# A selective scan beside a mixture of experts on one core: one of eight C products per step goes to GpSimd, small copies go to ScalarE, the preparation of dt moves half a step earlier

## The chip, the core and the metric

The kernel runs on one core of a Trainium2 chip. A core has five engines that run their own instruction streams in order and meet through semaphores: TensorE (PE, with its weight loads PEld), VectorE (DVE), ScalarE (ACT), GpSimd (POOL) and SyncE (SP), which here only issues DMAs. The metric is the device time of one execution in microseconds (us). Before the change the median of three executions is 4128.31 us (4123.35 to 4130.89).

## The reference, cut to what matters

All of it is in float32. Two branches work on the layer-normalised rows `xn` (16 x 1024 rows of 256) and are added to `x`.

```
x  = L0_attn_x                       # (16, 1024, 256)
xn = layernorm(x)
# branch 1: a selective scan, 32 states for each of 256 channels
dt = softplus(xn @ dt_w + dt_b);  b = xn @ B_w.T + B_b;  c = xn @ C_w.T + C_b
A  = -exp(log_A)                                     # (256, 32)
h_t = exp(A * dt_t) * h_(t-1) + (dt_t * x_t) * b_t   # (256, 32) for each row t
y_t = sum over states of h_t * c_t  +  D_skip * x_t
# branch 2: mixture of experts, 8 experts, 2 chosen per row, capacity 4096 rows each
out_e = relu(disp_e @ w1_e + b1_e) @ w2_e + b2_e;    moe_t = sum of 2 gates * out[expert, slot]
return x + y + moe
```

## The kernel before

A first part (about 370 us) normalises the rows, writes them to `xn_rows`, transposes them, routes them to experts and prepares dt, dt*x, b and c of the first batch entry. The rest is one loop of 128 steps, and everything below is about that loop. A batch entry has 1024 rows, done in two halves of 512 columns (`HALF`), and a half takes 4 steps (`ng` = 0 to 3). One step does two things side by side.

*The scan.* A step covers 8 groups of states (`k` = 0 to 7), each with two tiles (`dh` = 0, 1) of 128 partitions (4 states x 32 channels) by 512 rows. For one tile ScalarE computes the decay `exp(a*dt)` into PSUM (`decay`, line 734), GpSimd has multiplied `u = dtx * b` for both tiles of a k (line 935), and VectorE runs the scan over the 512 rows (line 1154). Then VectorE multiplies both tiles of h with c (`weigh`, line 1138, into `hc`), and TensorE sums the states of two k at a time into PSUM (`quad(s)` for k = 2s and 2s+1, line 569). There are two PSUM tiles for decays, so `decay` of a (k, dh) waits for the scan of (k-1, dh). `u` has four buffers, so GpSimd's product for k waits for the scans of k-4. h is a ring of four k and hc another: `weigh(k)` writes where k-4 stood and waits for the quad that read it.

*The experts.* Each step takes 256 slots of an expert: GpSimd gathers their rows (line 878), TensorE transposes them (`turn_slots`), multiplies with w1 (`moe_up(0..3)`, line 607) and w2 (`moe_down(0..1)`, line 623), ScalarE moves each PSUM tile on (`up_out`, line 769; `down_out`, line 778), and GpSimd scatters the result into the output in the next step with an adding DMA (line 895). GpSimd also adds y to the output (line 900, four DMAs per half, one per step) and forms the two small gate operands (lines 952 and 957).

*The preparation.* Each step also prepares 128 rows for a later half: TensorE's `prep` (line 527), ScalarE's `evac_prep`, `softplus` and `log_part` (lines 711 to 725), VectorE's `prep_dt` (line 1063), GpSimd's `dtx_part` (line 857), and SP stores them.

The order of each stream is written out by hand in Python loops; there is no scheduler. What matters below is what stands behind what. On TensorE one step is moe_up(0), moe_up(1), quad(0), moe_up(2), moe_up(3), quad(1), moe_down(0), prep, quad(2), moe_down(1), turn_slots, quad(3). On ScalarE the decays of k+1 follow the scans of k, and between them stand the other tasks by their k: `down_out(0)` stands behind the decays that follow k = 5, and so ahead of both decays for k = 7. On VectorE `weigh(k-1)` stands behind the first scan of k.

## Time and profile before

| | before |
|---|---|
| median of three executions | 4128.31 us |
| profiled execution, its own time | 4136.54 us |
| profiled execution, its span | 4134.7 us |
| VectorE busy | 3945.4 us (95%) |
| GpSimd busy | 3438.1 us (83%) |
| TensorE busy | 3386.1 us (82%) |
| ScalarE busy | 2479.6 us (60%) |
| mean granted TensorE clock | 0.915 |

The span runs from the first to the last instruction of the profiled execution. Busy time is an average over the set-up and the loop, and says nothing about which engine a step ends on; for that the time line of a single step has to be read. On GpSimd the record of an instruction can begin while the one before it still runs, so the mean duration of a group is longer than what one instruction adds to the engine's time. There the distance between two ends is the number to use.

### The profile page before, as it was taken

To read this page: it belongs to the slowest core of one execution; us is meant where nothing else is said; L and a number is where in the kernel's file an instruction comes from. 1 tells how busy PE (TensorE), PEld (TensorE's weight loads), DVE (VectorE), ACT (ScalarE), POOL (GpSimd) and SP (SyncE) were. 2 spreads that over 40 slices of the span, in tenths; PEclk is the share of its full clock that TensorE was granted. 3 is DMA by queue.
4 is the path that set the end of the run, shared out by engine and by line. 5 is a ranking of instruction groups with operands and counts; after the bars stand their busy time and mean duration, and the time that the engine had idled before them with its cause. 6 is when DMAs were issued, how large, how long until landed. Compare 5 with 4: busy or idle time off the path is not lost.

```text
span 4134.7 us, 75470 instructions
## 1 busy us (share of the span) xinstructions
PE 3386.1 (82%) x16264; PEld 2230.3 (54%) x16264; DVE 3945.4 (95%) x4035; ACT 2479.6 (60%) x5211; POOL 3438.1 (83%) x2340
## 2 busy tenths in 40 slices
PE   6788888878888888888888888888888888888786
PEld 3366555555555555555555555555555555555554
DVE  8797999999999999999999999999999999999997
ACT  2302666666666666666666666666666666666665
POOL 3003999989999899989998898988998999989997
PEclk8998999999999999999999999999999999999998
DMA  7983554445544454445554444445554544545554
GB/s 231 340 145 88 112 122 104 105 111 129 126 113 115 110 120 105 106 111 129 122 117 112 112 116 103 111 110 129 120 120 105 117 107 109 116 110 131 120 120 107
DMA packets 405229, 510.41 MB, mean 123 GB/s; under 512 B 71855, under 2 KB 242995, under 8 KB 404595
## 3 DMA queue, kind: packets, MB, share of 16 engines
q1 hardware_dynamic: 310774, 404.45, 36.0%
q0 software_dynamic: 68976, 84.86, 13.7%
q10 hardware_dynamic: 25104, 16.91, 1.8%
q8 instruction: 136, 2.23, 0.2%
q14 instruction: 239, 1.96, 0.2%
HBM read 381.48 MB, written 142.08 MB: 127 GB/s over the span
## 4 chain that ended last, share of the span: by engine, by line
DVE 32%; issue 15%; ACT 15%; PE 11%; POOL 11%; DVEq 4%; SPq 3%; DMA 3%; ACTq 1%; POOLq 0%
DVE h L1154 19%; ACT bank L734 11%; DVE hc L1138 10%; POOL u L935 6%; PE bank L623 4%; POOL out_rows L895 4%; PE bank L607 3%; DVEq L1154 3%; PE bank L569 2%; SPq L341 2%; ACT bank L785 2%; DMA dt<-dt_rows 1%; DVE hc L1116 1%; SPq L328 1%; ACT zv L711 1%
## 5 line engine op out<-in xcount | busy, mean ns | idle before, releaser
L935 POOL TENSOR_TENSOR u<-dtx,b_sb 128x1024 f32<-128x1024 f32 x1024 | 2656.9, 2785 | 139.3 <-DVE h L1154 125.4
L1154 DVE TENSOR_TENSOR_SCAN h<-bank,carry,u 128x512 f32<-128x512 f32 x2048 | 2541.1, 1276 | 107.9 <-ACT bank L734 81.0
L734 ACT ACTIVATE bank<-dt,a_neg 128x512 f32<-128x512 f32 x2050 | 1412.8, 690 | 1110.8 <-DVE h L1154 1048.9
L1138 DVE TENSOR_TENSOR hc<-h,bank 128x1024 f32<-128x1024 f32 x1024 | 1232.9, 1204 | 4.4
L607 PE MATMUL bank<-xgt,w_sb 128*128 128x256 f32 x4096 | 1109.7, 431 | 65.1 <-ACT ht L769 51.5
L607 PEld LDWEIGHTS bank<-xgt,w_sb 128*128 128x128 f32 x4096 | 871.8, 219 | 453.7 <-issue 317.3
L569 PE MATMUL bank<-hc,rsum 128*32 128x512 f32 x4096 | 618.7, 679 | 565.5 <-DVE hc L1138 563.2
L623 PE MATMUL bank<-w_sb,ht 128*128 128x256 f32 x4096 | 984.9, 395 | 0.0
L623 PEld LDWEIGHTS bank<-w_sb,ht 128*128 128x128 f32 x4096 | 780.2, 196 | 328.1 <-issue 226.2
L769 ACT ACTIVATE ht<-bank,b_sb 128x256 f32<-128x256 f32 x1024 | 423.8, 465 | 173.6 <-PE bank L607 160.8
L569 PEld LDWEIGHTS bank<-hc,rsum 128*32 128x32 f32 x4096 | 83.8, 112 | 752.2 <-DVE hc L1138 724.4
L895 POOL DMA_INDIRECT out_rows<-o_sb,sidx x258 | 414.7, 1607 | 66.4 <-issue 58.5
L857 POOL TENSOR_TENSOR dtx_n<-dt_n,xnt 128x256 f32<-128x256 f32 x136 | 173.9, 1279 | 300.5 <-DVE dt_n L1063 300.5
L878 POOL DMA_INDIRECT xg<-xn_rows,gidx x256 | 277.5, 1084 | 156.0 <-DVE h L1154 114.9
L900 POOL DMA_DIRECT2D out_rows<-y_sb x133 | 200.4, 1522 | 7.3 <-DMA out_rows<-o_sb,sidx 7.3
L785 ACT ACTIVATE bank<-c_sb 128x512 f32<-128x512 f32 x256 | 151.1, 590 | 14.5 <-DVE hc L1138 13.8
L711 ACT ACTIVATE zv<-bank,dtb 128x128 f32<-128x128 f32 x272 | 83.0, 356 | 126.4 <-PE bank L527 99.5
L527 PE MATMUL bank<-xnt,dtw 128*128 x1096 | 158.0, 287 | 0.0
L778 ACT ACTIVATE o_sb<-bank,gate 128x256 f32<-128x256 f32 x256 | 117.0, 457 | 51.7 <-PE bank L626 49.2
L527 PEld LDWEIGHTS bank<-xnt,dtw 128*128 128x128 f32 x1096 | 132.8, 191 | 17.0 <-issue 1.6
L554 PE MATMUL bank<-hc,u 128*128 128x256 f32 x512 | 119.3, 391 | 13.3 <-DVE hc L1116 13.3
L885 POOL COPY sidx<-slot_dst 128x2 int32 x129 | 121.3, 940 | 0.0
(109 smaller groups left out, 1960.6 us busy)
## 6 DMA issues: line engine op xcount, KB each, us to landing
dt<-dt_rows SPq DMA_DIRECT2D x528, 128.0 KB, 4.0
dtx<-dtx_rows SPq DMA_DIRECT2D x528, 128.0 KB, 3.4
b_sb<-bc_rows SPq DMA_DIRECT2D x520, 128.0 KB, 3.3
c_sb<-bc_rows SPq DMA_DIRECT2D x520, 128.0 KB, 3.5
w_sb<-w SPq DMA_DIRECT2D x18, 1024.0 KB, 7.6
dt_rows<-dt_n SPq DMA_DIRECT2D x136, 128.0 KB
dtx_rows<-dtx_n SPq DMA_DIRECT2D x136, 128.0 KB
out_rows<-y_sb POOLq DMA_DIRECT2D x133, 128.0 KB, 3.8
```

The source lines that it names most:

```text
L527: mm = pe.matmul(dst, w[:, k, :], src, start=(k == 0), stop=(k == KD - 1))
L569: mm = pe.matmul(y_ps[c * RD:(c + 1) * RD, s % 2, :], rsum[:], hc[:, 2 * (k % HB) + dh, :], start=False, stop=True, skip_group_check=True, ...
L607: mm = pe.matmul(m[:, c * SL:(c + 1) * SL], w1_sb[:, eo, kk, ch * P:(ch + 1) * P], xgt[:, kk, :], start=(kk == 0), stop=(kk == KD - 1))
L623: pe.matmul(m[:, 0:D], ht[:, c, j * P:(j + 1) * P], w2_sb[:, eo, c, :], start=(c == 0), stop=False)
L734: act.activation(a_ps[dh], dt[:, g, :], ACT.Exp, scale=a_neg[:, bass.ds(col, 1)]).then_inc(a_ready, 1)
L769: ins = act.activation(ht[:, ch, :], m_ps[f % 2][:, c * SL:(c + 1) * SL], ACT.Relu, bias=b1_sb[:, bass.ds(e * HC + ch, 1)])
L785: act.activation(c_ps, c_sb[:, ng % 2, jj, :], ACT.Copy).then_inc(c_ready, 1)
L878: pool.indirect_dma_start(xg[:, j, :], None, xn_d, rows, bounds_check=T - 1, oob_is_err=False).then_inc(xg_in, 16)
L895: pool.indirect_dma_start(outf, rows, o_sb[:, buf, j, :], None, bounds_check=T - 1, oob_is_err=False, compute_op=ALU.add).then_inc(o_scatt ...
L935: pool.tensor_tensor(u[:, 2 * i:2 * i + 2, :], dtx[:, 2 * gp:2 * gp + 2, :], b_sb[:, odd, k // 4, :].unsqueeze(1).to_broadcast([P, KD, HALF]),
L1138: dve.tensor_tensor(hc[:, 2 * (k % HB):2 * (k % HB) + 2, :], h[:, 2 * k % HR:2 * k % HR + 2, :], c_ps.unsqueeze(1).to_broadcast([P, KD, HA ...
L1154: dve.tensor_tensor_scan(h[:, (2 * k + dh) % HR, :], a_ps[dh], u[:, 2 * (k % UB) + dh, :], carry[:, bass.ds(hh % 2, 1), bass.ds(ng * 2 * N ...
```

## The change

1. The product of h with c for k = 3 (`HP = 3`) is done by GpSimd and no longer by VectorE. GpSimd reads c from SBUF. It stands behind GpSimd's u product for k = 7. VectorE's first scan of k = 7 waits for it (it overwrites those tiles of h), and so does TensorE's quad(1).
2. The gate products and the copies of the index columns `gidx` and `sidx` go from GpSimd to ScalarE, behind its decays of k = 2 (gates, gather index) and k = 6 (scatter index). The gate products become four activations of one column.
3. The four adding DMAs of y per half, of 128 rows each, become one of 512 rows, in the step with `ng` = 1.
4. The gathered rows have two buffers. The gathers stand behind GpSimd's k = 0 and k = 1, the scatters behind k = 4 and 5, `dtx_part` behind k = 3.
5. The preparation moves by about half a step: `prep` stands ahead of quad(1) on TensorE, `evac_prep` at k = 4, softplus at 5 and the logarithm at 6 on ScalarE, `prep_dt` behind the last scan of the step on VectorE. One more block is prepared ahead of the loop.
6. SP's stores and loads follow suit; `load_c` also waits for GpSimd's product.

```diff
@@ tensor @@
                             def quad(s):
-                                pe.wait_ge(hc_done, st * NG + 2 * s + 1 + 2)
+                                pe.wait_ge(hc_done, st * (NG - 1) + 2 * s + 1 - (2 * s + 1 >= HP) + 2)
+                                if s == HP // 2:
+                                    pe.wait_ge(hcp_done, st + 1)
                                 sum_states(s)
...
                                 quad(0)
                                 moe_up(2)
                                 moe_up(3)
+                                prepare()
                             quad(1)
                             moe_down(0)
-                            pe.wait_ge(xnt_in, 16 * (nx // HPB + 2))
-                            settle(pe)
-                            prep(NG + nx, 1 - nx // NG % 2, nx % NG)
                             quad(2)
@@ scalar @@
+                        def gates_in():
+                            act.wait_ge(xg_in, 16 * SJ * (st + 1))
+                            settle(act)
+                            for j in range(SJ):
+                                ins = act.activation(gate2[:, j:j + 1], xg[:, ng % 2, j, D + 1:D + 2], ACT.Copy,
+                                                     scale=slot_k[:, bass.ds(st * SJ + j, 1), 1])
+                            ins.then_inc(gate_mul, 1)
+                            act.wait_ge(gate_mul, st + 1)
+                            settle(act)
+                            for j in range(SJ):
+                                ins = act.activation(gate[:, j:j + 1], xg[:, ng % 2, j, D:D + 1], ACT.Identity,
+                                                     scale=slot_k[:, bass.ds(st * SJ + j, 1), 0], bias=gate2[:, j:j + 1])
+                            ins.then_inc(gate_ready, 1)
...
+                                if k == 5:
+                                    softplus(p)
+                                if k == 6:
+                                    log_part(p)
...
                             if k == 2:
-                                softplus(p)
-                                log_part(p)
+                                gates_in()
+                                lay_gather()
                             if k == 3:
                                 up_out(3)
+                            if k == 6:
+                                lay_scatter()
+                            if k == 4:
+                                evac_prep(p)
                             if k == 5:
                                 down_out(0)
@@ gpsimd @@
-            def add_y(hf, j):
-                pool.dma_start(outf.rearrange("(i p) d -> i p d", p=P)[bass.ds(hf * TB + j, 1)]
-                               .rearrange("a p d -> (a p) d"), y_sb[:, j, :], accum_op=ALU.add).then_inc(y_out, 16)
+            def add_y(hf):
+                pool.dma_start(groups(outf)[bass.ds(hf, 1)].rearrange("a p j d -> (a p) j d"), y_sb[:],
+                               accum_op=ALU.add).then_inc(y_out, 16)
...
+                            if k < 2:
+                                gather(st + 1, 1 - odd, k)
                             if k == 3:
                                 dtx_part(p, par, q)
+                            if k in (4, 5):
+                                scatter(st, 1 - odd, k - 4, hf + 1 if ng == 1 else None)
+                            if k == UB + HP:
+                                pool.wait_ge(c_in[odd], 16 * R * (hf * HPB // 2 + ng // 2 + 1))
+                                pool.wait_ge(nsum_done, st * 4 + HP // 2 - 2 + 1 + NSUM0)
+                                pool.wait_ge(scan_done, st * 2 * NG + 2 * HP + 2 + SCAN0)
+                                pool.tensor_tensor(hc[:, 2 * HP:2 * HP + 2, :], h[:, 2 * HP:2 * HP + 2, :],
+                                                   c_sb[:, odd, 0, :].unsqueeze(1).to_broadcast([P, KD, HALF]),
+                                                   ALU.mult).then_inc(hcp_done, 1)
@@ vector @@
+            prep_dt(NG)
...
+                                if (k, dh) == (HP + UB, 0):
+                                    dve.wait_ge(hcp_done, st + 1)
...
-                                if dh == 0 and k > 0:
+                                if dh == 0 and k > 0 and k - 1 != HP:
                                     weigh(st, k - 1)
-                            if k == 3:
-                                prep_dt(NG + st)
+                        prep_dt(NG + 1 + st)
                         weigh(st, NG - 1)
```

The first place is GpSimd in a step, from k = 5 on. This is before:

```order
L957 TENSOR_TENSOR gate<-gate 128x2
L873 REGISTER_ALU
L878 DMA xg<-xn_rows,gidx 128x258
L933 REGISTER_ALU
L935 TENSOR_TENSOR u<-dtx,b_sb 128x1024
L878 DMA xg<-xn_rows,gidx 128x258
L892 REGISTER_ALU
L895 DMA out_rows<-o_sb,sidx 16384x256
L933 REGISTER_ALU
L935 TENSOR_TENSOR u<-dtx,b_sb 128x1024
L895 DMA out_rows<-o_sb,sidx 16384x256
```

Now, from its u product for k = 4 on:

```order
L971 TENSOR_TENSOR u<-dtx,b_sb 128x1024
L924 ISA
L929 DMA out_rows<-o_sb,sidx 16384x256
L969 REGISTER_ALU
L971 TENSOR_TENSOR u<-dtx,b_sb 128x1024
L929 DMA out_rows<-o_sb,sidx 16384x256
L969 REGISTER_ALU
L971 TENSOR_TENSOR u<-dtx,b_sb 128x1024
L969 REGISTER_ALU
L971 TENSOR_TENSOR u<-dtx,b_sb 128x1024
L988 ISA
L990 TENSOR_TENSOR hc<-h,c_sb 128x1024
```

The h-by-c product (line 990) is the last of the step and has all four u products of k = 4 to 7 and both scatters ahead of it; the gate addition (line 957) and the gathers are gone from this stretch.

The second place is TensorE between moe_up(3) (lines 607 and 613) and moe_down(0) (lines 623 and 629), in a step with `ng` above 0. Before, with `rsum` marking a quad and `dtw` and `bcw` the preparation:

```order
L607 MATMUL bank<-xgt,w_sb 128x256 x4
L630 REGISTER_ALU
L569 MATMUL bank<-hc,rsum 32x512 x4
L615 REGISTER_ALU
L623 MATMUL bank<-w_sb,ht 128x256 x6
L621 REGISTER_ALU
L623 MATMUL bank<-w_sb,ht 128x256 x2
L626 MATMUL bank<-b_p,ones 128x256
L649 ISA
L521 REGISTER_ALU
```

Now:

```order
L613 MATMUL bank<-xgt,w_sb 128x256 x4
L527 REGISTER_ALU
L533 MATMUL bank<-xnt,dtw 128x128 x4
L533 MATMUL bank<-xnt,bcw 64x128 x2
L575 MATMUL bank<-hc,rsum 32x512 x4
L621 REGISTER_ALU
L629 MATMUL bank<-w_sb,ht 128x256 x6
L627 REGISTER_ALU
L629 MATMUL bank<-w_sb,ht 128x256 x2
L632 MATMUL bank<-b_p,ones 128x256
L575 MATMUL bank<-hc,rsum 32x512 x4
```

The preparation went ahead of quad(1); quad(1) still stands ahead of the whole of moe_down(0).

The third place is ScalarE in the same step around `down_out(0)` (the activation into `o_sb`). Before, from the decays for k = 6:

```order
L734 ACTIVATE bank<-dt,a_neg 128x512
L790 REGISTER_ALU
L734 ACTIVATE bank<-dt,a_neg 128x512
L775 ISA
L777 REGISTER_ALU
L778 ACTIVATE o_sb<-bank,gate 128x256
L822 ACTIVATE carry<-h 128x4
L790 REGISTER_ALU
L734 ACTIVATE bank<-dt,a_neg 128x512
```

Now (the decay is line 750 here):

```order
L750 ACTIVATE bank<-dt,a_neg 128x512
L732 ACTIVATE za<-zv 128x256
L734 ACTIVATE ze<-za 128x256
L830 REGISTER_ALU
L750 ACTIVATE bank<-dt,a_neg 128x512
L792 REGISTER_ALU
L793 ACTIVATE o_sb<-bank,gate 128x256
L868 ACTIVATE carry<-h 128x4
L830 REGISTER_ALU
L750 ACTIVATE bank<-dt,a_neg 128x512
L738 ACTIVATE bank<-ze 128x256
```

Parts of softplus came in, and `down_out(0)` stands where it stood: ahead of the first decay for k = 7.

## Rows read from the trace of the kernel before

**Rows 1.** Costliest groups of the page: line, engine, operation | busy us, mean ns | idle before.
```profile
L935 POOL TENSOR_TENSOR u<-dtx,b_sb 128x1024 f32<-128x1024 f32 x1024 | 2656.9, 2785 | 139.3 <-DVE h L1154 125.4
L1154 DVE TENSOR_TENSOR_SCAN h<-bank,carry,u 128x512 f32<-128x512 f32 x2048 | 2541.1, 1276 | 107.9 <-ACT bank L734 81.0
```

**Rows 2.** Time line of VectorE: start us, length us, what [idle before <-releaser].
```profile
397.97 0.42 DVE L1063 SCALAR_TENSOR_TENSOR dt_n<-zv,bank 128x256 f32<-128x256 f32 x1
...
2073.93 3.62 DVE L1154 TENSOR_TENSOR_SCAN h<-bank,carry,u 128x512 f32<-128x512 f32 x3
...
2080.96 1.20 DVE L1138 TENSOR_TENSOR hc<-h,bank 128x1024 f32<-128x1024 f32 x1
...
2085.55 1.28 DVE L1154 TENSOR_TENSOR_SCAN h<-bank,carry,u 128x512 f32<-128x512 f32 x1
2086.74 0.40 DVE L1063 SCALAR_TENSOR_TENSOR dt_n<-zv,bank 128x256 f32<-128x256 f32 x1
...
2096.31 2.46 DVE L1154 TENSOR_TENSOR_SCAN h<-bank,carry,u 128x512 f32<-128x512 f32 x2
...
2099.79 1.29 DVE L1154 TENSOR_TENSOR_SCAN h<-bank,carry,u 128x512 f32<-128x512 f32 x1
...
2102.26 3.63 DVE L1154 TENSOR_TENSOR_SCAN h<-bank,carry,u 128x512 f32<-128x512 f32 x3
```

**Rows 3.** All writers of dt_n: length min/median/max ns, first and last start.
```profile
L1063 DVE SCALAR_TENSOR_TENSOR dt_n<-zv,bank x136: 396/403/464, 246.8 to 4097.6; 128x256 f32<-128x256 f32 x136
```

**Rows 4.** Time line of GpSimd over a part of two steps.
```profile
2111.93 1.14 POOL L878 DMA_INDIRECT xg<-xn_rows,gidx  x1 [1.05 <-DVE h L1154]
...
2118.06 2.93 POOL L935 TENSOR_TENSOR u<-dtx,b_sb 128x1024 f32<-128x1024 f32 x1
2121.17 1.59 POOL L895 DMA_INDIRECT out_rows<-o_sb,sidx  x1 [0.17 <-DVE h L1154]
2122.20 1.31 POOL L857 TENSOR_TENSOR dtx_n<-dt_n,xnt 128x256 f32<-128x256 f32 x1
2122.89 7.57 POOL L935 TENSOR_TENSOR u<-dtx,b_sb 128x1024 f32<-128x1024 f32 x3
2129.82 1.55 POOL L900 DMA_DIRECT2D out_rows<-y_sb  x1
```

**Rows 5.** Time line of TensorE in the step of rows 2.
```profile
2082.21 1.94 PE L569 MATMUL bank<-hc,rsum 128*32 128x512 f32 x8 [3.42 <-DVE hc L1138]
2084.07 4.36 PE L607 MATMUL bank<-xgt,w_sb 128*128 128x256 f32 x16
2089.50 1.06 PE L569 MATMUL bank<-hc,rsum 128*32 128x512 f32 x8 [1.07 <-DVE hc L1138]
2094.15 0.28 PE L626 MATMUL bank<-b_p,ones 3*128 x1
2095.45 0.65 PE L527 MATMUL bank<-xnt,bcw 128*64 x4
```

**Rows 6.** Time line of ScalarE behind that moe_down(0).
```profile
2094.79 0.45 ACT L778 ACTIVATE o_sb<-bank,gate 128x256 f32<-128x256 f32 x1
2095.33 0.69 ACT L734 ACTIVATE bank<-dt,a_neg 128x512 f32<-128x512 f32 x1
```

**Rows 7.** Time lines of TensorE, ScalarE and VectorE in a step with ng = 0.
```profile
2031.38 1.94 PE L569 MATMUL bank<-hc,rsum 128*32 128x512 f32 x8 [2.81 <-DVE hc L1138]
2033.25 5.86 PE L623 MATMUL bank<-w_sb,ht 128*128 128x256 f32 x16
...
2039.35 0.47 ACT L778 ACTIVATE o_sb<-bank,gate 128x256 f32<-128x256 f32 x1 [2.62 <-PE bank L626]
...
2040.79 1.28 DVE L1154 TENSOR_TENSOR_SCAN h<-bank,carry,u 128x512 f32<-128x512 f32 x1 [1.30 <-ACT bank L734]
```

**Rows 8.** Time lines of TensorE and ScalarE around one preparation ahead of the loop.
```profile
344.57 1.09 PE L527 MATMUL bank<-xnt,dtw 128*128 x8
...
347.93 0.39 ACT L725 ACTIVATE bank<-ze 128x256 f32<-128x256 f32 x1
```

More of the change, by code:

```diff
@@ L154, in ssm_moe @@
         sidx = sb("sidx", [P, SJ], I32)
-        xg = sb("xg", [P, SJ, D + 2])
-        gate2 = sb("gate2", [P, SJ, 2])
+        xg = sb("xg", [P, 2, SJ, D + 2])
+        gate2 = sb("gate2", [P, SJ])
+        HP = 3
         gate = sb("gate", [P, SJ])
@@ L443, in _ @@
                         settle(sp)
+                        sp.wait_ge(hcp_done, st + 1)
+                        settle(sp)
                         load_c(ng % 2, st + 2)
-                        store_dtx(p, par, q)
+                        nxt = hh * HPB + ng + 1
+                        store_bc(p + 1, (1 + nxt // NG) % 2, nxt % NG)
                         if last:
@@ L730, in _ @@
                 log_part(q)
+            evac_prep(NG)
+            softplus(NG)
+            log_part(NG)
             def decay(dh, col, g):
@@ L877, in gather @@
                 rows = bass.IndirectOffsetOnAxis(ap=gidx[:, j:j + 1], axis=0)
-                pool.indirect_dma_start(xg[:, j, :], None, xn_d, rows,
+                pool.indirect_dma_start(xg[:, buf, j, :], None, xn_d, rows,
                                         bounds_check=T - 1, oob_is_err=False).then_inc(xg_in, 16)
-            def lay_scatter(st):
-                pool.wait_ge(o_scattered, 16 * SJ * (st + 1))
-                settle(pool)
-                pool.tensor_copy(sidx[:], slot_dst[:, bass.ds(st * SJ, SJ)]).then_inc(sidx_done, 1)
             def scatter(st, buf, j, added):
                 if j == 0:
-                    pool.wait_ge(sidx_done, st + 2)
+                    pool.wait_ge(sidx_done, st + 1)
                     pool.wait_ge(evac_done, st * FS + 1)
-                    pool.wait_ge(y_out, 16 * added)
+                    if added is not None:
+                        pool.wait_ge(y_out, 16 * added)
                     settle(pool)
@@ L908, in _ @@
                 rows = bass.IndirectOffsetOnAxis(ap=gidx[:, j:j + 1], axis=0)
-                pool.indirect_dma_start(xg[:, j, :], None, xn_d, rows,
+                pool.indirect_dma_start(xg[:, 0, j, :], None, xn_d, rows,
                                         bounds_check=T - 1, oob_is_err=False).then_inc(xg_in, 16)
+            pool.wait_ge(xg_in, 16 * SJ)
+            pool.tensor_copy(gidx[:], slot_tok[:, 2 * SJ:3 * SJ]).then_inc(gidx_done, 1)
             pool.wait_ge(map_ready, 2)
@@ L937, in _ @@
                                                ALU.mult).then_inc(u_ready, 1)
-                            if k == 2:
-                                pool.wait_ge(y_evac, hf + (2 if ng > 0 else 1))
+                            if k == 0 and ng == 1:
+                                pool.wait_ge(y_evac, hf + 2)
                                 pool.wait_ge(o_scattered, 16 * SJ * (st + 1))
                                 settle(pool)
-                                if ng > 0:
-                                    add_y((hf + 2 * B - 1) % (2 * B), ng - 1)
-                                else:
-                                    add_y((hf + 2 * B - 2) % (2 * B), TB - 1)
+                                add_y((hf + 2 * B - 1) % (2 * B))
@@ L955, in _ @@
-                            if k == 5:
-                                pool.wait_ge(gate_mul, st + 1)
-                                pool.tensor_tensor(gate[:], gate2[:, :, 0], gate2[:, :, 1], ALU.add).then_inc(gate_ready, 1)
-                                gather(st + 1, 0)
-                            if k == 6:
-                                gather(st + 1, 1)
-                                scatter(st, 1 - odd, 0, st + 1)
-                            if k == 7:
-                                scatter(st, 1 - odd, 1, st + 1)
-                                dtx_part(p, par, q)
@@ L966, in _ @@
-            pool.wait_ge(o_scattered, 16 * SJ * (STEPS + 1))
-            add_y(2 * B - 2, TB - 1)
-            lay_scatter(STEPS)
+                                dtx_part(p, par, q)
+                            if k in (4, 5):
[7 more added lines that the diff above has]
+                                                   ALU.mult).then_inc(hcp_done, 1)
@@ L969, in _ @@
             for j in range(SJ):
-                scatter(STEPS, 1, j, STEPS + 1)
+                scatter(STEPS, 1, j, None)
             pool.wait_ge(o_scattered, 16 * SJ * (STEPS + 2))
             pool.wait_ge(y_evac, 2 * B + 2)
-            for j in range(TB):
-                add_y(2 * B - 1, j)
-            pool.wait_ge(y_out, 16 * (STEPS + 1 + TB))
+            add_y(2 * B - 1)
+            pool.wait_ge(y_out, 16 * (2 * B + 1))
             pool.wait_ge(xg_in, 16 * SJ * (STEPS + 1))
```

70 lines of the change are left out of this document (35 added, 35 removed).

## The prediction

> **What bounds the kernel now.** I read the page's first and fifth part, then the time line of one step on VectorE, then those of the engines that VectorE waits for, then the same in a step that was longer. The page says that VectorE is 95% busy and that its scan group sat idle for 107.9 us in all, 81.0 of them for ScalarE's decays [rows 1]. On the time line a step without a stall runs from the scan at 2073.93 to the one at 2102.26, which is 28.33 us [rows 2]; it holds 16 scans of 1.18 us (3.63 for three, less the 0.10 by which records overlap), 8 weighs of 1.11 and the 0.31 of dt_n. The first dt_n of the loop starts at 397.97 [rows 2] and the last at 4097.6 [rows 3], 127 steps apart, so a mean step is (4097.6 - 397.97)/127 = 29.13 us. So 0.80 us per step are stalls, and VectorE sets the time. If GpSimd takes one weigh, VectorE needs 28.33 - 1.11 = 27.22.
>
> GpSimd is the next to look at. Three u products end 7.57 - 0.62 = 6.95 us after dtx_n ends (2123.51 to 2130.46), which is 2.32 each [rows 4], not the 2.785 of the page [rows 1]; the records overlap the instruction ahead. A scatter behind a product adds 1.77 (2120.99 to 2122.76), dtx_n 0.75 (2122.76 to 2123.51), a gather 1.14 and about 0.17 ahead of it, and the first gather has 1.05 us of idle time ahead of it, for the gate it waits for [rows 4].
>
> **The change part by part.** The h-by-c product has the shape and operands (two in SBUF) of u, so I take 2.35 us for it; it and u are the same form, and between u's own extremes there is little room (2.32 when back to back, 2.37 at most with a wait ahead). GpSimd's step is then 9 products, 21.0, two gathers 2.5, two scatters 3.55 and dtx_n 0.75: 27.8 us, plus add_y. It loses four tiny instructions (0.13 each) and the 1.05 of idle time. So GpSimd alone could run a step in 27.8, VectorE in 27.2, both under 28.33. That would be the gain. It is lost to order.
>
> Follow h of k = 3. Call t the end of its second scan (2085.55 + 1.28 = 2086.83 in the step shown [rows 2]). Before, weigh(3) followed within one scan, TensorE started quad(1) at 2089.50, the last matmul of moe_down(0) ended at 2094.43, ScalarE's down_out(0) started at 2094.79 and the first decay for k = 7 ended at 2096.02 [rows 5, 6], 1.46 us before its scan began at 2096.31 + 1.17 = 2097.48 [rows 2]. Now GpSimd must do u for k = 7 and the product, 4.7 us and 0.2 for the wait: the product ends at t + 4.9 at the earliest, call that T. From T on everything is in order behind one another: quad(1) and moe_down(0) 4.93 (2089.50 to 2094.43), down_out(0), carry and decay 1.2 (2094.79 to 2096.02), and the hand-overs 0.1 from GpSimd and 0.28 to VectorE (2039.35 + 1.16 = 2040.51 to 2040.79 [rows 7]). That is 6.5 us from T to the first scan of k = 7. Between t and that scan VectorE now has six scans and two weighs, 6 x 1.18 + 2 x 1.11 = 9.3, so it would start it at t + 9.3. It can start it at t + 4.9 + 6.5 = t + 11.4. VectorE waits 2 us in every step, behind k = 6, for ScalarE, and the 1.42 us saved are gone.
>
> Now close the circle. From the first scan of k = 7 to the first scan of the next step is 2102.26 - 2097.48 = 4.78 [rows 2], and 0.31 for dt_n, which moves there: 5.09. The next u for k = 4 waits for both scans of k = 0: 5.09 + 2.46 + 0.2 = 7.75. From there GpSimd has u 2.35, scatter 1.77, u 2.35, scatter 1.77, u 2.32, u 2.32, the product 2.35: 15.3, so the next product ends 23.1 behind the first scan of k = 7. The step is 23.1 + 6.5 = 29.6 us. With GpSimd always on time it would be 5.09 + 12.90 (2073.93 to 2086.83) + 4.9 + 6.5 = 29.4, so GpSimd is late by 0.2 only. Against the mean of 29.13 the loop loses 0.47 x 128 = 60 us. The present stalls of 0.80 us do not come on top: those behind k = 4 to 6 fall into the new 2 us wait, and the longer work of TensorE at ng = 0 into its wait for the product.
>
> add_y: four DMAs of 1.55 us become one, of which no row has the size. From below it costs no more than one of 128 rows, 1.55 [rows 4]; from above four times that, 6.2. Between T and the u of k = 4 GpSimd has 3 x 2.32 + 2.6 = 9.5 ahead of u for k = 3, which may start at 6.5 + 3.6 + 0.2 = 10.3, and ends with dtx_n at 13.4 where the next u may start at 14.25: 1.7 us of room. At 1.55 it costs nothing, at 6.2 it costs 4.5 x 32 = 144 us. I take 2.5, nearest to the row that is there, and 0.8 x 32 = 26 us. By the Trainium skill, DMA: Bandwidth & Descriptors, Anatomy of one DMA, descriptor generation is small and many descriptors can be emitted before more of them cost anything; by that this term would be 0. No row here has two sizes to test it.
>
> TensorE's clock: quad(1) takes 1.06 us where the engine idled 1.07 ahead, and 1.94 with 2.81 or 3.42 of idle time ahead; behind the 2.81 the moe_down took 5.86 us, and from quad(1) to the scan it was 2040.79 - 2031.38 = 9.41 us [rows 5, 7], 2.8 more than the warm 6.6. That step is also the model of what I expect: VectorE stalled for 1.30 us there for the same decay [rows 7]. In the new order TensorE is through with the preparation 5.09 + 8.23 (end of weigh(1), 2082.16 [rows 2]) + 6.2 + 1.8 = 21.3 behind the first scan of k = 7 (quad(0) to moe_up(3) 2082.21 to 2088.43 [rows 5]), the product comes at 23.1, so it idles 1.8, nearer to the 1.07. With add_y in the step it is 2.6 and may go either way; I take a quarter of 32 x 2.8, some 20 us.
>
> Gates and index copies on ScalarE: about 6 x 0.2 us, where the softplus of 1.3 us left; each decay behind them has its scan a group later, so nothing. If that cover were gone it would be 0.2 x 128 = 26 us. The second gather buffer takes a wait for moe_up(0) off the gathers and costs nothing. SP's load_c waits for the product, with half a step and more in hand; nothing. Ahead of the loop one preparation more stands between the last count and the slot maps: 344.57 to 348.32 on TensorE and ScalarE [rows 8], 3.75, and dt_n, hand-overs and a store: 6 us.
>
> Sum: 60 + 26 + 20 + 6 = 112 on the profiled execution's own 4136.5 (its span is 4134.7). That execution is 8.2 us over the median of 4128.3, so the forecast is 4128.3 + 112 = 4240.
>
> **The rivals.** *GpSimd's sum decides and nothing is late (faster).* A step of 27.8 and add_y 2.5/4 = 0.6 gives 28.4: 0.73 x 128 = 93 less and 6 more, 4041. It holds if the product is out by t + 2.9, so that the decay for k = 7 is where VectorE wants it. For it: GpSimd's sum and VectorE's are both below 28.33. Against it: u for k = 7 alone takes until t + 2.5, and the three orders all put moe_down(0) behind quad(1) and the decay behind down_out(0).
>
> *No change.* The circle at its shortest, 29.4, no add_y, no cold quad: 0.27 x 128 + 6 = 41 above before at most; to come to nothing TensorE would have to pass from quad(1) to the last matmul in 4.6 in place of 4.93. For it: quad(2) and quad(3) steps run at the full clock. Against: the 4.93 are at the full clock already.
>
> *The cold circle (slower by more).* The idle time ahead of quad(1) is enough to drop the clock in most steps, from 2.4 to 1.2 GHz. Then 2.8 us come on top in each such step. At add_y 6.2 and in a quarter of the steps: 4128 + 60 + 144 + 90 + 6 = 4428. In all steps it would be over 4500. For it: 2.81 us of idle time did it in [rows 7]. Against: the 1.8 us I work out.
>
> **How the numbers follow.** Forecast and its neighbours, 4165 to 4320: 0.60. Faster rival: 0.15. No change and little more, 4120 to 4165: 0.12. Cold circle or dear add_y, above 4320: 0.13. The range for 8 in 10 leaves out most of the first rival and the worst of the last: 4085 to 4350. Below 0.2% (8 us) no change can be told from none: faster 0.16, same 0.06, slower 0.78.
>
> **What would show it.** In the profile after, the scan of k = 7 has about 2 us of idle time ahead, released by ScalarE's decay, in nearly every step, 200 us and more in all; ScalarE's down_out(0) waits for TensorE in nearly every step; quad(1) waits for GpSimd's product. The step is 29.6 where dt_n starts are compared. VectorE's busy time falls by 128 x 1.2 = 154 us and its share to about 90%. The product takes 2.35 us. I am wrong if VectorE's idle time stays below 100 us, if the product stands behind less than u for k = 7, or if add_y takes over 3 us.

## The result, and the profile after

| | before | after |
|---|---|---|
| median | 4125.83 us | 4357.20 us |
| ratio to before, 95% interval | | 1.0552 (1.0536 to 1.0568) |
| profiled execution, span | 4134.7 us | 4358.9 us |
| VectorE busy | 3945.4 us (95%) | 3808.9 us (87%) |
| GpSimd busy | 3438.1 us | 3581.2 us |
| mean granted TensorE clock | 0.915 | 0.897 |

The change makes the kernel 5.5% slower; the medians are 231 us apart, the two profiled executions 224 us (4358.9 against 4134.7). The sign and the place were as forecast, but the loss is twice the 112 us of the sum, and 7 us beyond the range.

Costliest groups of the page after. The first line answers to that of VectorE's scan in [rows 1]:

```profile
L1181 DVE TENSOR_TENSOR_SCAN h<-bank,carry,u 128x512 f32<-128x512 f32 x2048 | 2534.3, 1270 | 474.4 <-ACT bank L750 448.4
L971 POOL TENSOR_TENSOR u<-dtx,b_sb 128x1024 f32<-128x1024 f32 x1024 | 2579.9, 2550 | 339.4 <-DVE h L1181 320.8
L1163 DVE TENSOR_TENSOR hc<-h,bank 128x1024 f32<-128x1024 f32 x896 | 1073.1, 1198 | 0.0
L793 ACT ACTIVATE o_sb<-bank,gate 128x256 f32<-128x256 f32 x256 | 118.8, 464 | 444.7 <-PE bank L632 428.4
L990 POOL TENSOR_TENSOR hc<-h,c_sb 128x1024 f32<-128x1024 f32 x128 | 325.2, 2540 | 0.0
```

ScalarE's `down_out` before, from the same part of the page:

```profile
L778 ACT ACTIVATE o_sb<-bank,gate 128x256 f32<-128x256 f32 x256 | 117.0, 457 | 51.7 <-PE bank L626 49.2
```

VectorE has 128 products fewer, and its idle time ahead of scans went from 107.9 to 474.4 us, nearly all of it until a decay of ScalarE. ScalarE's `down_out`, which waited 51.7 us in the kernel before, now waits 444.7, for TensorE. And GpSimd itself waits for VectorE, 320.8 us: in this kernel no engine's own work is the bound.

The chain in one step is the one to look at. Time lines of the changed kernel on VectorE, GpSimd, TensorE and ScalarE, one fence each:

```profile
2116.25 1.28 DVE L1181 TENSOR_TENSOR_SCAN h<-bank,carry,u 128x512 f32<-128x512 f32 x1 [2.41 <-ACT bank L750]
...
2142.39 1.28 DVE L1181 TENSOR_TENSOR_SCAN h<-bank,carry,u 128x512 f32<-128x512 f32 x1
2147.21 1.28 DVE L1181 TENSOR_TENSOR_SCAN h<-bank,carry,u 128x512 f32<-128x512 f32 x1 [3.54 <-ACT bank L750]
```
```profile
2131.66 5.22 POOL L971 TENSOR_TENSOR u<-dtx,b_sb 128x1024 f32<-128x1024 f32 x2
2136.64 2.54 POOL L990 TENSOR_TENSOR hc<-h,c_sb 128x1024 f32<-128x1024 f32 x1
...
2141.24 1.60 POOL L934 DMA_DIRECT2D out_rows<-y_sb  x1
```
```profile
2108.28 1.52 PE L575 MATMUL bank<-hc,rsum 128*32 128x512 f32 x8 [1.97 <-POOL hc L990]
2109.73 4.91 PE L629 MATMUL bank<-w_sb,ht 128*128 128x256 f32 x16
...
2139.23 1.75 PE L575 MATMUL bank<-hc,rsum 128*32 128x512 f32 x8 [4.07 <-POOL hc L990]
2140.91 4.68 PE L629 MATMUL bank<-w_sb,ht 128*128 128x256 f32 x16
2145.53 0.28 PE L632 MATMUL bank<-b_p,ones 3*128 x1
```
```profile
2145.84 0.47 ACT L793 ACTIVATE o_sb<-bank,gate 128x256 f32<-128x256 f32 x1 [4.93 <-PE bank L632]
2146.21 0.20 ACT L868 ACTIVATE carry<-h 128x4 f32<-128x4 f32 x1
2146.31 0.68 ACT L750 ACTIVATE bank<-dt,a_neg 128x512 f32<-128x512 f32 x1
```

Read them as a circle. From the first scan of k = 7 (2116.25) to the end of GpSimd's product (2139.18) it is 22.93 us. TensorE begins quad(1) 0.05 later, ends moe_down(0) at 2145.81, ScalarE takes down_out(0), carry and the decay, and the next scan of k = 7 begins at 2147.21, 8.03 behind the product: 30.96 us in all. VectorE was ready for it 3.54 us earlier. The two quads show the part that I mis-sized: with 1.97 us of idle time ahead quad(1) took 1.52 us, with 4.07 it took 1.75, and the moe_down behind it 4.9 and 4.7. In the step of [rows 5] quad(1) took 1.06 at 2.4 GHz, and the moe_down behind it, in the kernel before, 3.72:

```profile
2090.50 3.72 PE L623 MATMUL bank<-w_sb,ht 128*128 128x256 f32 x16
```

The granted clock of the changed kernel was 0.58 of full speed from 2139.2 to 2141.0 and 0.80 from 2141.0 to 2145.8.

The mean step, from the first dt_n of the loop to the last (all writers of dt_n in the second fence), is (4341.9 - 423.25)/127 = 30.86 us against 29.13:

```profile
419.75 1.28 DVE L1181 TENSOR_TENSOR_SCAN h<-bank,carry,u 128x512 f32<-128x512 f32 x1 [9.31 <-ACT bank L750]
...
423.25 0.39 DVE L1087 SCALAR_TENSOR_TENSOR dt_n<-zv,bank 128x256 f32<-128x256 f32 x1
```
```profile
L1087 DVE SCALAR_TENSOR_TENSOR dt_n<-zv,bank x137: 392/396/421, 245.9 to 4341.9; 128x256 f32<-128x256 f32 x137
```

127 x 1.73 = 220 us of the 224 between the two profiled executions lie between these marks, and 5 us ahead of the first dt_n and behind the last: the stretch ahead grew from 397.97 to 423.25 us, mostly since dt_n now stands at the end of its step, and the one behind shrank from 37.1 to 17.0. In the very first step the chain held the scan of k = 7 back by 9.31 us.

### The profile page after: what moved, and what is told of

Its sections match the earlier page's. It is cut to its first block, busy times and chain, and to the rows that moved or that the text cites. A ratio compares the mean times of both kernels' runs of the same rounds, so it can differ in the third digit from the quotient of the medians.

```text
span 4358.9 us, 74834 instructions
## 1 busy us (share of the span) xinstructions
PE 3471.6 (80%) x16264; PEld 2278.4 (52%) x16264; DVE 3808.9 (87%) x3908; ACT 2612.1 (60%) x5985; POOL 3581.2 (82%) x1856
## 4 chain that ended last, share of the span: by engine, by line
PE 23%; issue 23%; DVE 19%; POOL 18%; ACT 11%; DVEq 2%; DMA 2%; SPq 1%; ACTq 0%; POOLq 0%
DVE h L1181 14%; PE bank L629 11%; POOL u L971 10%; ACT bank L750 6%; POOL hc L990 6%; PE bank L575 5%; PE bank L613 3%; DVE hc L1163 3%; PE bank L560 3%; ACT ht L784 2%; POOL out_rows L929 2%; DMA dt<-x 1%; DVEq L1181 1%; DVE h L1055 1%; ACT bank L738 1%
## 5 line engine op out<-in xcount | busy, mean ns | idle before, releaser
L1181 DVE TENSOR_TENSOR_SCAN h<-bank,carry,u 128x512 f32<-128x512 f32 x2048 | 2534.3, 1270 | 474.4 <-ACT bank L750 448.4
L971 POOL TENSOR_TENSOR u<-dtx,b_sb 128x1024 f32<-128x1024 f32 x1024 | 2579.9, 2550 | 339.4 <-DVE h L1181 320.8
L575 PE MATMUL bank<-hc,rsum 128*32 128x512 f32 x4096 | 670.8, 731 | 759.0 <-DVE hc L1163 473.9
L613 PE MATMUL bank<-xgt,w_sb 128*128 128x256 f32 x4096 | 1083.4, 422 | 15.4 <-issue 11.8
L1163 DVE TENSOR_TENSOR hc<-h,bank 128x1024 f32<-128x1024 f32 x896 | 1073.1, 1198 | 0.0
L629 PE MATMUL bank<-w_sb,ht 128*128 128x256 f32 x4096 | 1067.7, 419 | 0.0
L629 PEld LDWEIGHTS bank<-w_sb,ht 128*128 128x128 f32 x4096 | 841.5, 211 | 385.7 <-issue 262.2
L793 ACT ACTIVATE o_sb<-bank,gate 128x256 f32<-128x256 f32 x256 | 118.8, 464 | 444.7 <-PE bank L632 428.4
L903 POOL TENSOR_TENSOR dtx_n<-dt_n,xnt 128x256 f32<-128x256 f32 x136 | 99.7, 733 | 299.7 <-DVE dt_n L1087 299.7
L990 POOL TENSOR_TENSOR hc<-h,c_sb 128x1024 f32<-128x1024 f32 x128 | 325.2, 2540 | 0.0
L533 PE MATMUL bank<-xnt,dtw 128*128 128x128 f32 (+1 forms) x1096 | 148.0, 278 | 0.0
L560 PEld LDWEIGHTS bank<-hc,u 128*128 128x128 f32 x512 | 95.5, 193 | 35.7 <-DVE hc L1140 23.6
```

Of the source, the lines that this page charges most:

```text
L533: mm = pe.matmul(dst, w[:, k, :], src, start=(k == 0), stop=(k == KD - 1))
L560: pe.matmul(map_ps, oh_p[:, r, :], oh_c[:, r, :], start=False, stop=True, skip_group_check=True).then_inc(oh_used, 1)
L575: mm = pe.matmul(y_ps[c * RD:(c + 1) * RD, s % 2, :], rsum[:], hc[:, 2 * (k % HB) + dh, :], start=False, stop=True, skip_group_check=True, ...
L613: mm = pe.matmul(m[:, c * SL:(c + 1) * SL], w1_sb[:, eo, kk, ch * P:(ch + 1) * P], xgt[:, kk, :], start=(kk == 0), stop=(kk == KD - 1))
L629: pe.matmul(m[:, 0:D], ht[:, c, j * P:(j + 1) * P], w2_sb[:, eo, c, :], start=(c == 0), stop=False)
L971: pool.tensor_tensor(u[:, 2 * i:2 * i + 2, :], dtx[:, 2 * gp:2 * gp + 2, :], b_sb[:, odd, k // 4, :].unsqueeze(1).to_broadcast([P, KD, HALF]),
```

## The experiments

All times are medians in us; "step" is the mean distance of dt_n starts in the profiled execution. e11_early and e12_product_alone were timed once and have no ratio. The kernel before was timed again beside each group.

| kernel | time | ratio to before | step |
|---|---|---|---|
| before | 4126 to 4133 | | 29.13 |
| after | 4357.20 | 1.0552 | 30.86 |
| e1_warm | 4222.21 | 1.0220 (1.0203 to 1.0237) | 29.79 |
| e2_swap | 4091.39 | 0.9903 (0.9886 to 0.9919) | 28.81 |
| e3_late_out | 4184.25 | 1.0127 (1.0110 to 1.0144) | 29.52 |
| e4_first | 4121.23 | 0.9972 (0.9959 to 0.9984) | 29.02 |
| e5_back | 4124.27 | 0.9996 (0.9984 to 1.0008) | 29.02 |
| e8_swap_early | 4062.69 | 0.9845 (0.9829 to 0.9862) | 28.51 |
| e10_back_early | 4070.75 | 0.9862 (0.9844 to 0.9881) | 28.64 |
| e11_early | 4393.40, one run | | 31.12 |
| e12_product_alone | 4803.14, one run | | 34.37 |
| e13_swap_early_dt | 4036.93 | 0.9769 (0.9753 to 0.9786) | 28.36 |
| e14_swap_early_dt_first | 4022.95 | 0.9732 (0.9716 to 0.9748) | 28.24 |

### e1_warm: fill TensorE's wait with work

```diff
-            def prep(p, par, q):
+            def prep(p, par, q, reps=1):
...
-                for g in range(3):
+                for g in list(range(3)) * reps:
...
-                                prep(NG + 1 + st, (1 + nxt // NG) % 2, nxt % NG)
+                                prep(NG + 1 + st, (1 + nxt // NG) % 2, nxt % NG, 3 if ng == 0 else 2)
```

> The changed kernel with the matmuls of the preparation ahead of quad(1) issued twice (three times where ng = 0), the same values each time: 1.7 us (3.4 us) more work for TensorE per step, laid into its wait for GpSimd's product. Theory (the missing 1.4 us per step are the clock that falls in that wait): quad(1) takes 1.06 in place of 1.5 to 1.75 us, moe_down(0) 3.7 in place of 4.7 to 4.9, from the end of the product to the first scan of k = 7 it is 6.5 in place of 8.0 us, the step falls from 30.9 to about 29.5 and the time to about 4185. Rival (TensorE is simply too full or late in the new order, the clock is not the cause): more work makes it no faster, 4357 to 4450.

135 us less by doing more. Time line of TensorE:

```profile
2136.49 0.65 PE L533 MATMUL bank<-xnt,bcw 128*64 128x128 f32 x4
2137.62 1.07 PE L575 MATMUL bank<-hc,rsum 128*32 128x512 f32 x8 [0.48 <-POOL hc L990]
2138.61 3.72 PE L629 MATMUL bank<-w_sb,ht 128*128 128x256 f32 x16
2142.27 0.28 PE L632 MATMUL bank<-b_p,ones 3*128 x1
```

quad(1) and moe_down(0) are back at 2.4 GHz (granted clock 1.00 from 2137.6 to 2142.5): 4.93 us from the start of the one to the end of the other. From the product to the scan of k = 7 the median is 6.48 us, against 8.12 in the changed kernel, and from that scan to the next product it stays (22.91 against 22.88). The median step is 29.38 us, the 29.4 of the circle with GpSimd on time.

The mean is 29.79, so the time came out 37 us above the expected 4185. In 37 steps the way from the product to the scan of k = 7 is longer, by 34 us in all, mostly since stalls of about 2.4 us ahead of the scans of k = 4 and 5 outlast the wait for the product; another 21 us lie between the scan and the product over the ends of the halves. The clock is the missing part, and the rival is out.

### e11_early: the same work, laid elsewhere

```diff
                             moe_up(1)
+                            if ng > 0:
+                                prepare()
...
-                                prepare()
                             quad(1)
```

> The changed kernel with the preparation ahead of quad(0) where ng is above 0, quad(1) still ahead of moe_down(0): the same work, moved. Theory (the clock in the wait for the product is the missing part of the step): the idle time ahead of quad(1) grows by the 1.7 us of the preparation, quad(1) takes 1.94 and moe_down(0) 5 to 6 us, the circle is 22.9 + 9.4 = 32.3 us in three steps of four, time 4480 to 4560. Rival (a constant hand-over or another order costs the missing part, not the clock): unchanged, 4340 to 4370, or faster as e8_swap_early was.

4393 is between the two. Time line of TensorE:

```profile
2119.31 1.06 PE L575 MATMUL bank<-hc,rsum 128*32 128x512 f32 x8 [3.43 <-POOL hc L991]
2120.31 5.41 PE L629 MATMUL bank<-w_sb,ht 128*128 128x256 f32 x16
```

Over each kernel I took the idle time ahead of the quad that waited for the product, and the time from its start to the end of moe_down(0), as medians over the 89 such steps of e1_warm and all 128 of the others:

| kernel | idle ahead | quad(1) to end of moe_down(0) |
|---|---|---|
| e1_warm | 0.43 us | 4.93 us |
| after | 1.98 | 6.57 |
| e11_early | 5.06 | 6.54 |
| e12_product_alone | 6.76 | 6.71 |

The medians hide two kinds of steps. In the changed kernel 31 of the 128 waits ahead of quad(1) were under 1.8 us, 17 of them in steps with ng = 1, and behind none of them was anything lost (4.93 us). Behind all of the other 97 it took 6.5 us or more, with 1.8 to 2.4 us ahead as with 4. In e11_early 125 of 128 steps lost that much. So the low clock mostly costs 1.6 to 1.8 us, with 2 us idle as with 7, and up to 3.1 in single steps (15 of 128 in e11_early lost more than 2); the 2.8 that I had read from one step in [rows 7] is such a one. What e11_early adds are the 28 steps that had been warm, 28 x 1.6 = 45 us, and this agrees with the 36 measured and not with the 130 to 200 expected. My sizes for both theories missed.

### e2_swap and e3_late_out: cut the chain at TensorE, or at ScalarE

```diff
e2_swap                              e3_late_out (ScalarE)
-                  quad(1)           -      if k == 5:
                   moe_down(0)       -          down_out(0)
+                  quad(1)                  if k == 6:
                   quad(2)           +          down_out(0)
                                                lay_scatter()
```

> The changed kernel with moe_down(0) ahead of quad(1) on TensorE, nothing else. Theory (the loss is the chain product, quad(1), moe_down(0), down_out(0), decay of k = 7): down_out(0) no longer waits for GpSimd, the scan of k = 7 has no idle time ahead beyond a few tenths, GpSimd's own work sets the step at 28.0 to 28.5, time 4010 to 4070, faster than before. Rival (GpSimd's product is late by itself and VectorE and TensorE wait for it in any order): over 4250.

> The changed kernel with ScalarE's down_out(0) behind the decays for k = 7 in place of ahead of them; TensorE's order as in the changed kernel. Theory: the same chain is cut at ScalarE; down_out(0) still waits for the product, quad(1) and moe_down(0), but now holds the decays of the next k = 0, one group (3.5 us) later, so the circle has 3 to 5 us more room and GpSimd's work sets the step, about 28.2 to 28.8, 4020 to 4100. Rival (TensorE's late quads hold VectorE's weighs, not ScalarE's order): 4300 or more.

Two calls in another order take 266 us away, and the kernel is 1% faster than before. Both rivals are out. The cut on ScalarE takes away 173. Time line of e3_late_out on ScalarE, with both of its down_outs waiting for TensorE in one step:

```profile
2125.49 0.47 ACT L793 ACTIVATE o_sb<-bank,gate 128x256 f32<-128x256 f32 x1 [1.18 <-PE bank L632]
...
2130.35 0.47 ACT L793 ACTIVATE o_sb<-bank,gate 128x256 f32<-128x256 f32 x1 [2.56 <-PE bank L632]
```

The wait went on to the second one. Over the run down_out(1) waits 278.0 us, which was nothing in the changed kernel, and down_out(0) 155.5 in place of 444.7. down_out(1) holds the decays for the next k = 1, and there VectorE now stands still: 196.0 of its 297.4 us of idle time ahead of scans, where the changed kernel had 9.5. Ahead of the scans of k = 0, where I had expected it, it is 26.5.

Both came in above their expectation (by 21 and 84 us). For e2_swap the time line tells why. VectorE in two steps, then TensorE in the second:

```profile
2117.19 0.40 DVE L1087 SCALAR_TENSOR_TENSOR dt_n<-zv,bank 128x256 f32<-128x256 f32 x1
...
2144.49 0.40 DVE L1087 SCALAR_TENSOR_TENSOR dt_n<-zv,bank 128x256 f32<-128x256 f32 x1
...
2161.64 1.28 DVE L1181 TENSOR_TENSOR_SCAN h<-bank,carry,u 128x512 f32<-128x512 f32 x1 [1.63 <-ACT bank L750]
```
```profile
2154.22 1.94 PE L575 MATMUL bank<-hc,rsum 128*32 128x512 f32 x8 [3.42 <-DVE hc L1163]
2156.08 5.56 PE L613 MATMUL bank<-xgt,w_sb 128*128 128x256 f32 x16
```

A step without a stall is 27.30 us, VectorE's own 27.2. The next one loses 1.63 us behind k = 3: quad(0), with its idle time of 3.42 us ahead as in [rows 5], runs at 1.2 GHz, moe_up(2) is late, and the decay for k = 4 stands behind its `up_out`. Weigh(3) on VectorE used to cover much of this wait: ahead of the scans of k = 4 and 5 VectorE is idle for 157 us in e2_swap, and for 63 in e5_back, where it has weigh(3).

27.30 is under the 27.8 that I had for GpSimd, but that does not refute the 27.8. `u` has four buffers, so in a single step VectorE can use up a lead of GpSimd. To see GpSimd's own work I took each step from the end of its first u product to that of the next, less the idle time that another engine or a DMA ended. It is 27.8 us as a median and 28.1 to 28.2 as a mean, which has add_y in it, in e2_swap and in all later versions with the product on GpSimd. What GpSimd waits comes on top: 2.6 us per step in the changed kernel, 0.6 in e2_swap. With this work on GpSimd no order can make the mean step shorter than about 28.1 us.

### e4_first: the product ahead of u for k = 7

```diff
+                            if k == UB + HP:
+                                ... (the product, as it is)
                             pool.wait_ge(scan_done, st * 2 * NG + 2 * (k - UB) + 2 + SCAN0)
                             pool.tensor_tensor(u[...], ...)
-                            if k == UB + HP: ...
```

> The changed kernel with GpSimd's h-by-c product ahead of its u product for k = 7 in place of behind it; both wait for the same scan. Theory: the product ends 2.35 us earlier, TensorE's idle time ahead of quad(1) goes and with it the low clock: 22.9 - 2.35 + 6.5 = 27.1 would be the circle, under GpSimd's own 27.8, so a step of 28.0 to 28.5 and 4010 to 4070. Rival (only the order matters, the clock does not recover): 22.9 - 2.35 + 8.0 = 28.6 and 4065 to 4110. Second rival (GpSimd's product is late whatever its place): over 4250.

236 us less, by two products that change places on one engine. It fell short of its expectation by 51, and is above the first rival too. 78 steps still waited for the product; in 25 of them the wait was 1.8 us or more, and quad(1) and moe_down(0) took 6.4 to 7.9 us in place of 4.93. The stalls behind k = 3 are here too: 128 us ahead of the scans of k = 4 and 5.

### e5_back and e12_product_alone: the two halves of the change

e5_back has the product on VectorE again and every other edit of the change; e12_product_alone is the kernel before with the product on GpSimd and nothing else:

```diff
e12_product_alone (on the kernel before, GpSimd; its waits left out, indices written out)
+                            if k == UB + HP:
+                                pool.tensor_tensor(hc[:, 6:8, :], h[:, 6:8, :], c_sb ..., ALU.mult).then_inc(hcp_done, 1)
                             if k == 7:
                                 scatter(st, 1 - odd, 1, st + 1)
```

> The changed kernel with the product for k = 3 back on VectorE, as before the change; all its other edits stay. Theory (the product's place in the chain is the whole loss, the other edits cost next to nothing): a step is near 28.4 to 29.3 as before, time 4080 to 4160, within 1% of before. Rival (the moved preparation, gates on ScalarE and the double buffer cost much of the 230 us by themselves): over 4200.

> The kernel before with one edit alone: GpSimd does the product for k = 3, behind its u product for k = 7, with the waits that go with it. Theory: the same chain with more ahead of the product (gate sums, 1.05 us of idle time, two gathers and one scatter between the u products for k = 4 and 7) and a longer idle time ahead of quad(1), since the preparation stands behind it: 24.8 + 9.4 = 34.2 us per step, time 4650 to 4800. Rival (effects add up: the product alone costs the 230 us of the change less what the rest costs): 4350 to 4450.

All the other edits together make no difference that can be measured (0.9996); whether one of them gains what another costs was not tested. The product alone costs 677 us, 3 above the expected 4650 to 4800. Time lines of TensorE, GpSimd and VectorE in e12_product_alone:

```profile
2127.04 1.93 PE L573 MATMUL bank<-hc,rsum 128*32 128x512 f32 x8 [6.69 <-POOL hc L973]
2128.90 4.72 PE L627 MATMUL bank<-w_sb,ht 128*128 128x256 f32 x16
```
```profile
2123.98 2.91 POOL L973 TENSOR_TENSOR hc<-h,c_sb 128x1024 f32<-128x1024 f32 x1
```
```profile
2100.97 1.28 DVE L1170 TENSOR_TENSOR_SCAN h<-bank,carry,u 128x512 f32<-128x512 f32 x1 [5.87 <-ACT bank L740]
...
2135.24 1.28 DVE L1170 TENSOR_TENSOR_SCAN h<-bank,carry,u 128x512 f32<-128x512 f32 x1 [5.88 <-ACT bank L740]
```

The step of 34.27 us here agrees with the expected 34.2, but by two errors that cancel: from scan to product it is 25.9 us (24.8 expected), from product to scan 8.35 (9.4). So the rest of the change is worth 446 us once the product is on GpSimd, and nothing without it: it shortens the way from the scan of k = 7 to the product from 25.9 to 22.9 us, and that way counts only while the circle is closed. Effects do not add here.

### e8_swap_early, e10_back_early, e13_swap_early_dt, e14_swap_early_dt_first: what is left

e8_swap_early is e2_swap with the edit of e11_early; e10_back_early is e5_back with it.

> e2_swap (4091.39) with TensorE's preparation ahead of quad(0) in place of behind moe_up(3), in the steps with ng above 0. Theory (what is left of the stalls in e2_swap is the clock that falls in the 3.42 us of idle time ahead of quad(0), which makes moe_up(2) late for the decay for k = 4): the idle time becomes 1.7 us, quad(0) takes 1.06 in place of 1.94, the stalls behind k = 3 go, a step is 27.3 to 27.7 and the time 3915 to 3970. Rival (GpSimd's own work, 27.8 and add_y, is the bound): 28.1, 4000 or more. Second rival (the clock still falls): 4080 to 4100.

> e5_back with the preparation ahead of quad(0) where ng is above 0: the product on VectorE, the clock kept up. Theory: VectorE's 28.33 us are the step and the stalls of 0.8 us mostly go; 28.4 to 28.6, 4030 to 4070. The distance to e8_swap_early is then what the product on GpSimd is worth once it is off the chain: 1.1 us x 128 = 140 us. Rival (the clock has nothing to do with the stalls of the kernel before): as e5_back.

e10_back_early came out at the upper edge of its expectation (4070.75). It has 36.4 us of stalls until a decay where e5_back had 73.6, and quad(0) took over 1.2 us in 6 steps in place of 85, so the clock ahead of quad(0) did cost the order before some 50 us. But the distance to e8_swap_early is 8 us and not 140. Once it is off the chain, the product on GpSimd is worth next to nothing: with it on VectorE that engine needs 28.2 to 28.3 us per step (28.33 in the kernel before, 28.18 in the shortest step here), and with it on GpSimd that one needs 28.1.

e8_swap_early missed its expectation by 93 us, and its first rival, GpSimd's own work of about 28.1, came nearest: GpSimd waits only 0.35 us per step. What is left sits at one place: three steps of four take 27.7 to 28.0, the one over the half's end 30.66. ScalarE, SyncE and GpSimd at such an end:

```profile
2106.20 0.69 ACT L751 ACTIVATE bank<-dt,a_neg 128x512 f32<-128x512 f32 x1 [4.71 <-DMA dt<-dt_rows]
```
```profile
2096.22 1.82 SPq L330 DMA_DIRECT2D c_sb<-bc_rows  x4
2098.15 0.48 SPq L354 DMA_DIRECT2D bc_rows<-bcv  x1
2098.89 4.56 SPq L343 DMA_DIRECT2D dt<-dt_rows  x8
```
```profile
2087.01 2.93 POOL L991 TENSOR_TENSOR hc<-h,c_sb 128x1024 f32<-128x1024 f32 x1
```

The loads of dt that the decays soon want stand behind load_c, and the change made load_c wait for GpSimd's product. When I wrote the next expectation I took that wait for the cause. It is not: the product ended at 2089.94, 6.3 us before load_c began, and at all 32 ends of halves load_c began over 5 us behind it. SyncE issues one load behind the other from 2077.16 to 2103.45, with no pause over 0.7 us, and the last loads of dt are late because of all that stands ahead of them in that queue. The edit takes them ahead of the loads of b and c:

```diff
                             dt_pair(1)
+                            dt_pair(2)
+                            dt_pair(3)
...
                         store_bc(p + 1, (1 + nxt // NG) % 2, nxt % NG)
-                        if last:
-                            dt_pair(2)
-                            dt_pair(3)
```

> e8_swap_early (4062.69) with SyncE's loads of dt for k = 2 and 3 of the next half ahead of its loads of b and c in place of behind them. Theory (what e8_swap_early lost are 2.7 us per half in ScalarE's wait for these loads, which stood behind load_c and so behind GpSimd's product): the step over the half's end falls from 30.7 to about 28, 85 us less, 3960 to 3990. Rival (the loads are late for another reason, bandwidth or the stores ahead): 4050 to 4070.

> e13_swap_early_dt with GpSimd's product ahead of its u product for k = 7. Theory (GpSimd's own work is the bound by now, and the product's place no longer is): the same as e13_swap_early_dt within 10 us. Rival (the product is still on the chain through quad(1) and the weighs): 20 to 60 us faster than e13_swap_early_dt.

26 us from that move, not 85. ScalarE's wait for dt fell from 82.3 to 6.1 us and the step over the half's end from 30.66 to 28.64, but the steps with ng = 2 and 3 grew by 0.8 and 0.4 us. The 3960 to 3990 that I expected would have needed steps shorter than GpSimd's own work: e13_swap_early_dt has a mean step of 28.36, of which GpSimd waits 0.23. What still waits is the old chain, one group of states later. TensorE, ScalarE and VectorE in one step:

```profile
2024.71 3.64 PE L574 MATMUL bank<-hc,rsum 128*32 128x512 f32 x16 [4.73 <-POOL hc L990]
```
```profile
2033.38 0.47 ACT L793 ACTIVATE o_sb<-bank,gate 128x256 f32<-128x256 f32 x1 [3.38 <-PE bank L631]
```
```profile
2035.45 1.28 DVE L1181 TENSOR_TENSOR_SCAN h<-bank,carry,u 128x512 f32<-128x512 f32 x1 [2.37 <-ACT bank L750]
```

quad(1) waits for the product, quad(2) and moe_down(1) stand behind it, down_out(1) waits for them and holds the decay for k = 1. Over the run down_out(1) waits 184.4 us, and 98.7 of VectorE's 149.6 us of idle time ahead of scans stand ahead of k = 1.

With the product ahead of u for k = 7 as well, that wait of down_out(1) falls to 114.3 us and the time to 4022.95, 14 us less, a difference between the two expectations. That version is 2.7% faster than the kernel before and the fastest of the study. It has come to the bound: its mean step is 28.24 us, of which GpSimd waits 0.11. It is 48 us under e10_back_early, which has the product on VectorE, keeps 0.3 us of stalls per step and lacks SyncE's edit. The page's line of its u products has 14.7 us of idle time, where the changed kernel had 339.4:

```profile
L979 POOL TENSOR_TENSOR u<-dtx,b_sb 128x1024 f32<-128x1024 f32 x1024 | 2624.0, 2642 | 14.7 <-DMA dtx<-dtx_rows 5.1
```

## Why the prediction was right on the side and wrong on the size

- *The chain.* Right, each link. The scan of k = 7 waits for the decay, that one for down_out(0), moe_down(0), quad(1) and the product. Cutting it on TensorE or ScalarE (e2, e3), shortening it (e4) or taking the product out of it (e5) gives back 173 to 266 us, against 231 us lost.
- *From the scan to the product, 23.1 us.* Measured 22.93 in the step shown, 22.88 as a median.
- *From the product to the scan, 6.5 us at full clock.* 6.5 in e1_warm, 8.0 to 8.1 in the changed kernel.
- *The clock, the step that failed.* The prediction put 20 us on it, "a quarter of 32 x 2.8", because the idle time ahead of quad(1) was worked out as 1.8 us, "nearer to the 1.07" that had done no harm. The idle time was right as a median (1.98). What it does was wrong: between 1.07 us without harm and 2.81 with it I took the near row for nearly all steps, and a wait of about 2 us already cost 1.6 us, in 97 of 128 steps. By e1_warm the clock is worth (30.86 - 29.79) x 127 = 136 us, nearly seven times the term.
- *The circle, 60 us.* By e1_warm (29.79 - 29.13) x 127 = 84. The circle itself was sized a little high: its median, 29.38, is 32 us above the mean step before. The long stalls ahead of k = 4 and 5, once covered by weigh(3), and the half's end came on top with 34 and 21 us, where I had let all present stalls vanish in the new wait.
- *add_y, 26 us.* From the end of the product ahead of it to its own end the DMA of 512 rows takes 1.35 us as a median, that of 128 rows took 0.91; the lengths of the records, 1.60 and 1.55 [rows 4], overlap what stands ahead. That is within the 1.7 us of room that I had worked out, and the step with add_y is the shortest of the four (30.38 us), so the term is 0. The Trainium skill's DMA: Bandwidth & Descriptors, Anatomy of one DMA, says that many descriptors can be emitted before the added cost shows. The trace agrees: four times the rows cost 0.44 us more.
- *Ahead of the loop, 6 us.* 5 measured ahead of the first dt_n and behind the last, with the first step's chain in it.
- *Gates on ScalarE, the double buffer.* No net cost together with the rest, by e5_back. *load_c behind the product.* Free, as forecast: in e8_swap_early too the product had ended over 5 us earlier where the loads of dt were late.
- *The rivals.* GpSimd's sum as the bound did not decide the changed kernel, where GpSimd waits 2.6 us per step. But the sum was right, 27.8, and with the chain out of the way it is what decides (e14_swap_early_dt_first, 4022.95, near this rival's 4041). The cold circle, given a part of 0.13, was the case that came true, in three quarters of the steps and at 1.6 us in most and not 2.8.

On the profiled executions 84 + 136 + 0 + 5 = 225 us, against 224 measured. The medians are 231 us apart, because the profiled execution before stood 10.7 us above its median and the one after 3.4 above its own. That the forecast sum missed by no more is in part luck: the 26 us of add_y, which cost nothing, made up for some of what the clock term lacked.

## What to carry to other kernels

Work moved off the busiest engine saves only if whoever reads its result can wait: follow the result through each in-order stream back to the engine it was taken from, close the circle, and compare it with that engine's own work. Compare it also with the work of the engine that takes it over. Here VectorE needed 28.3 us per step, and GpSimd with the product needs 28.1, so the move by itself had some 0.2 us per step to give, 26 us in all, and the order was worth ten times that (266 us in e2_swap). A wait on TensorE can cost twice, for itself and for the clock behind it, so a wait should fall behind the urgent matmuls. When two edits act on one circle, test them together, since alone one can be worth nothing and the other cost three times as much.

## What the runs showed of the hardware

- Waits of about 2 us cost nearly as much in clock as waits of 7: behind all 97 waits of 1.8 us or more ahead of quad(1) in the changed kernel, quad(1) and moe_down(0) took 6.5 us or more against 4.93. quad(1) alone, 1.49 us as a median against 1.06 and 1.94, shows only a part of it, since the granted clock often fell while it ran or behind it (in the step shown of e11_early quad(1) took 1.06 and the moe_down 5.41).
- The length of a wait alone does not tell. With 2.0 to 2.4 us ahead of quad(1) all 23 cases of the changed kernel lost, but only 17 of 73 in e10_back_early; with 1.6 to 1.8 ahead 14 of 23 lost in e3_late_out and none of 23 in e4_first. In the kernel before none of the 284 quads with under 1.6 us ahead was slow, and 96 of the 119 with 2.4 us or more were. What decides between them was not followed up.
- The loss stayed small against the wait: 1.6 to 1.8 us as a median over a quad and a moe_down, whether 2 or 7 us were idle ahead (6.5 to 6.7 against 4.93), and 3.1 at most.
- More work on TensorE kept its clock up: repeating 1.7 us of matmuls per step shortened the step by 1.07 us.
- An adding DMA issued by GpSimd added 1.35 us to that engine's time with 512 rows of 1 KB, and 0.91 with 128 rows.
